# A graph-attention layer's last chunks: four of them smaller, one more of them, and their softmax chain in one piece

## What is computed

```python
def _gat_layer(x, src, dst, edge_attr_full, W, att, b, ew, eb):
    edge_emb = edge_attr_full @ ew.T + eb
    xw = x @ W
    xj = xw[src].reshape(-1, H, D) + edge_emb.reshape(-1, H, D)
    xi = xw[dst].reshape(-1, H, D)
    alpha = jnp.einsum('ehd,hd->eh', xi, att_i) + jnp.einsum('ehd,hd->eh', xj, att_j)
    alpha = jax.nn.leaky_relu(alpha, NEG_SLOPE)
    amax = jax.ops.segment_max(alpha, dst, num_segments=N)
    ea = jnp.exp(alpha - amax[dst])
    denom = jax.ops.segment_sum(ea, dst, num_segments=N)
    alpha = ea / (denom[dst] + EPS)
    msg = xj * alpha[..., None]
    aggr = jax.ops.segment_sum(msg, dst, num_segments=N)
    return aggr.mean(axis=1) + b
```

## Time and profile before

| | |
|---|---|
| median of three runs | 3343.92 us |
| the profiled execution's own time | 3336.89 us |
| its span, first to last instruction | 3335.0 us |
| TensorE busy | 2402.9 us, 72% of the span |
| GpSimd busy | 2172.8 us, 65% |
| VectorE busy | 2021.6 us, 61% |
| ScalarE busy | 669.5 us, 20% |
| the chain that ended last: GpSimd, VectorE, TensorE, issue, DMA | 30%, 28%, 22%, 13%, 4% |

### The profile page before, as it was taken

How to read it: one execution, slowest core, us unless ns; L and a number is a source line. 1 busy time by engine, 2 the same in 40 slices (tenths; PEclk the granted TensorE clock), 3 DMA queues, 4 the chain that set the end, 5 groups by cost and what they waited for, 6 DMA issues and landing times.

```text
span 3335.0 us, 48601 instructions
## 1 busy us (share of the span) xinstructions
PE 2402.9 (72%) x13595; PEld 1979.9 (59%) x13595; DVE 2021.6 (61%) x6441; ACT 669.5 (20%) x3102; POOL 2172.8 (65%) x2357
## 2 busy tenths in 40 slices
PE   6879955777675677668477777747777685777668
PEld 6669924566564566556366565636556573556557
DVE  8965464665565565656655665755665574665557
ACT  0048921111114111110411111131111122111112
POOL 0047737777755777774677777377777737777772
PEclk9555555555557555555755555575555566555556
DMA  3211112222221222221222222122222212222221
GB/s 100 102 66 68 46 55 59 60 61 58 63 48 43 58 63 58 58 64 40 50 63 58 58 67 56 33 59 61 58 60 64 56 35 57 60 60 58 58 55 50
DMA packets 114123, 195.78 MB, mean 59 GB/s; under 512 B 39898, under 2 KB 77273, under 8 KB 113865
## 3 DMA queue, kind: packets, MB, share of 16 engines
q0 software_dynamic: 62560, 130.25, 17.4%
q1 hardware_dynamic: 51304, 62.42, 5.9%
HBM read 180.86 MB, written 11.67 MB: 58 GB/s over the span
## 4 chain that ended last, share of the span: by engine, by line
POOL 30%; DVE 28%; PE 22%; issue 13%; DMA 4%; DVEq 2%; ACT 1%; POOLq 0%; ACTq 0%
POOL ring L510 28%; PE bank L745 10%; PE bank L747 5%; DMA ring<-table,srci 4%; DVE acc L1208 2%; PE bank L718 2%; DVE into L1149 2%; PE bank L741 2%; DVE prod L1072 2%; DVE ring L847 2%; DVE lanes L1135 2%; DVE fwd L1156 1%; POOL ring L491 1%; PE bank L783 1%; DVEq L1016 1%
## 5 line engine op out<-in xcount | busy, mean ns | idle before, releaser
L510 POOL DMA_INDIRECT ring<-table,srci x1955 | 1903.9, 974 | 633.1 <-issue 571.4
L745 PE MATMUL bank<-pw,ring 128*128 128x48 f32 x3910 | 1216.9, 411 | 0.0
L745 PEld LDWEIGHTS bank<-pw,ring 128*128 128x128 f32 x3910 | 1009.1, 316 | 103.8 <-issue 23.9
L741 PE MATMUL bank<-zeros 128*128 128x288 bf16 x490 | 209.6, 428 | 622.0 <-DVE pw L1167 622.0
L747 PE MATMUL bank<-onehot,est 128*36 128x24 f32 x3910 | 619.1, 246 | 0.0
L747 PEld LDWEIGHTS bank<-onehot,est 128*36 128x36 f32 x3910 | 382.6, 150 | 177.5
L586 ACT ACTIVATE dd<-dd 128x66 f32<-128x66 f32 x75 | 19.4, 258 | 2152.2 <-DVE dd L1160 2152.2
L741 PEld LDWEIGHTS bank<-zeros 128*128 128x128 bf16 x490 | 54.3, 111 | 665.3 <-DVE pw L1167 630.7
L1111 DVE TENSOR_TENSOR alpha<-alpha,ring 128x56 f32<-128x56 f32 (+7 forms) x75 | 18.1, 241 | 702.6 <-DMA ring<-table,srci 702.4
L1208 DVE TENSOR_TENSOR acc<-acc,bank 128x288 f32 x490 | 222.4, 454 | 301.7 <-PE bank L747 183.0
L580 ACT COPY ai_win<-ai_rows 128x48 f32 x1955 | 309.1, 228 | 58.0 <-issue 22.7
(11 more groups left out here) (214 smaller groups left out, 2676.1 us busy)
## 6 DMA issues: line engine op xcount, KB each, us to landing
ring<-table,srci POOLq DMA_INDIRECT x1955
ai_rows<-lo_dram SPq DMA_DIRECT2D x28, 896.0 KB, 4.3
at<-in_attr SPq DMA_DIRECT2D x65, 224.0 KB, 2.5
table<-ring SPq DMA_DIRECT2D x15, 390.0 KB, 3.6
table<-ring SPq DMA_DIRECT2D x5, 325.0 KB, 3.3
result<-ring SPq DMA_DIRECT2D x24, 64.0 KB
x_mid<-ring SPq DMA_DIRECT2D x3, 384.0 KB, 2.7
table<-ring SPq DMA_DIRECT2D x5, 130.0 KB, 2.3
```

The lines of the kernel that those rows point to most:

```text
L510: nc.gpsimd.indirect_dma_start(out=ring[:, slot(t), :], out_offset=None, in_=table, in_offset=bass.IndirectOffsetOnAxis(ap=srci[:, t:t + 1 ...
L741: nc.tensor.matmul(total, zeros[:, 0:P], zeros[:, :], start=True, stop=False, skip_group_check=True)
L745: nc.tensor.matmul(wide[:, 0:H, at_k], ring[:, slot(t), 0:D], pw[:, g % DEEP, k, :, :], start=False, stop=False, skip_group_check=True)
```

## The change

The list of chunks becomes eleven of 28 tiles and then 24, 20, 16, 12 and 11, sixteen in all; the number of groups stays 98. The ring has 59 slots, since the flags of one more chunk need the room of one. `FULL` is 11, the first smaller chunk. While chunks 0 to 10 are worked on, the order on VectorE is as before. In chunks 11 to 14 all of `windows_sum` for the next chunk runs ahead of add 0, and its chain runs in one piece ahead of the third add from the end, that is behind 3, 2, 1 and 0 adds. The chain's end then weighs three groups of chunks 12 to 15, and the end of the chunk the fourth where there is one. `ROW_BLOCKS` has six blocks in place of three.

```diff
-CH = [K] * 13 + [16, 11]
+CH = [K] * 11 + [24, 20, 16, 12, 11]
 NC = len(CH)
+FULL = CH.count(K)
...
-RING = 60
+RING = 59
...
-def chain_at(c):
-    return (2, 3, 5) if len(GC[c]) >= 7 else (0, 1, len(GC[c]) - 2)
+CHAIN = (2, 3, 5)
+
+
+def chain_before(c):
+    return len(GC[c]) - 3 if c >= FULL else None
+
+
+def weighed_early(c):
+    return 2 if c <= FULL else min(3, len(GC[c]))
...
-        ROW_BLOCKS = [(0, 13, K), (13, 14, CH[13]), (14, 15, CH[14])]
+        ROW_BLOCKS = [(0, FULL, K)] + [(c, c + 1, CH[c]) for c in range(FULL, NC)]
...
-                for g in GC[c][0:2 if c else AHEAD]:
+                for g in GC[c][0:weighed_early(c) if c else AHEAD]:
                     weigh(layer, g)
...
-                    scan_at, rows_at, probs_at = chain_at(c)
+                    scan_at, rows_at, probs_at = CHAIN if chain_before(c) is None else (None, None, None)
                     n_groups = len(GC[c])
                     for i, g in enumerate(GC[c]):
-                        if more and scan_at >= 2 and i < 3:
+                        if more and scan_at is not None and i < 3:
                             windows_sum(layer, c + 1, i)
+                        if more and scan_at is None and i == 0:
+                            for part in range(3):
+                                windows_sum(layer, c + 1, part)
+                        if more and i == chain_before(c):
+                            chain_scan(layer, c + 1)
+                            chain_rows(layer, c + 1)
+                            chain_cols(layer, c + 1)
+                            chain_probs(layer, c + 1)
                         add_group(layer, g)
...
-                        if more and scan_at < 2 and i == 0:
-                            for part in range(3):
-                                windows_sum(layer, c + 1, part)
...
-                            for ahead in GC[c + 1][2:AHEAD]:
+                            for ahead in GC[c + 1][weighed_early(c + 1):AHEAD]:
                                 weigh(layer, ahead)
```

## The result

The changed kernel takes 3308.01 us (median of four runs, 3305.78 to 3308.75) against 3344.14 for the kernel before: ratio 0.9891, 95% interval 0.9874 to 0.9908, 36.1 us less. The forecast was 3304, the range 3295 to 3318. The profiled execution takes 3305.78 us, its span is 3303.9.

What follows compares the result with a forecast made beforehand. GpSimd's gathers set the pace, but the change reaches each layer's tail, a string of VectorE work: 8.3 us a layer, 41.6 over five, less 1.5 for slower gathers, 40.1 off, so 3304 us against the median; range 3295 to 3318.

Steps and rivals of the forecast that it cites:

- the tail: End of each layer, last gather to last add: 31.99 us in layer 1, forecast to fall to near 23.7.
- VectorE's string: Layer 1 from chunk 13's landing at 947.55: VectorE's work alone sets the last add, 997.5, 8.3 us before 1005.84.
- The rival of a tail that does not move: End of each layer: held adds stop TensorE, or the last chain still starts near 985.7; 3344 us, 4%.
- half of the gain: Rival for the whole kernel: a mixture, with only half of the forecast saving, 3324 us; 4%.
- The sum: Whole kernel: 41.6 us saved over five layers less 1.5 is 40.1 us off 3336.89, giving 3296.8.
- gathers beside a denser VectorE: One more chain lies under gathers: charged 0.3 us a layer, 1.5 in all; bounds 0 and 4.2 a layer.
- The rival of the gathers slowed by 4.2 us a layer: VectorE's copies lock GpSimd out of the port, delaying every landing: 21 us in all, 3323 us; 8%.
- VectorE a chunk behind: Rival at chain 13: VectorE comes to it late, so the 16th chunk is added work; 16 us slower, 3360; 6%.
- The offset to the median: Kernel before: its profiled execution, 3336.89, is 7.0 us below the median 3343.92; carried over, 3296.8 becomes 3304.
- Ring 59: Gathers ask for slots one tile, 1.25 us, sooner; some 20 us cover it, else up to 1.25 us a layer.
- SP's row loads: Prologue: 36 issues become 72, with 2.8 us of cover for the look-up copy; taken as 0, bounds 0 and +2 us.
- The held adds: Chunks 11 to 14: adds held behind the chain keep PSUM, but six banks suffice, so TensorE goes on; no cost.

Runs made afterwards that it cites:

- the early and late doubling: Changed kernel with the second window-sum reduction run three times: early for chunks 12 and 13, 3305.91 us; late for chunks 14 and 15, 3320.26 us.
- side by side: No edit: the changed kernel and the kernel before, measured again in one series on one chip: 3306.21 against 3344.51 us, ratio 0.9886.
- the sizes alone: New chunk sizes and ring of 59 with the old order on VectorE, against the kernel before: 3339.13 us, ratio 0.9983.
- the copies beside gathers: Changed kernel with four extra SBUF copies of 128 x 672 float32 in VectorE's wait ahead of the chains of chunks 1 to 10: 3317.89 us, one execution.
- the wait put to use: Changed kernel with the first two parts of chunk 14's window sums, and ScalarE's copies for them, moved ahead of chain 13: 3298.24 us, ratio 0.9857.
- the shorter order alone: Changed kernel with the old sizes and ring of 60, so only chunk 13's loop has the new order: 3331.15 us, ratio 0.9963 against the kernel before.

## Why the prediction was right

- **The bound and the place.** GpSimd paces, the tail is VectorE's string, it begins at chunk 13's landing: shown by the early and late doubling. The rival of a tail that does not move is out (39.40 to 31.35 us of idle time), and so is that of half the gain.
- **The string's terms**, forecast and then measured in layer 1: chain 12 9.3 and 9.34; chain 13 9.12 and 9.06; weighings, adds, weighing and rescale 3.40 and 3.40 (958.92 to 962.32); sums of chunk 14 with its one add 4.03 and 4.35 (to 966.67); chain 14 8.6 and 8.86; 3.13 and 3.15; sums of chunk 15 2.93 and 2.93; chain 15 8.65 and 8.52; 0.41 and 0.41; 9.67 and 9.67. From chunk 13's landing to the last add 49.95 and 50.35. The largest miss is the add ahead of chain 14, for which I took the 0.56 us of idle time seen ahead of other adds; it has 0.91, ended by TensorE's sum. The next is chain 14, 0.26 us.
- **The sum.** The tail gave 40.6 us where the forecast had 41.6. The medians gave 36.1 and 38.3 in two series, where I had 40.1. The profiled pairs put the tail at 40.6 and 41.1, so the missing 2 to 4 us are not in the tail; the gathers' pace, which moved one execution by 11 us, is large enough for them, but the executions at the medians were not profiled. The range has a slip: 1.3 us a layer are 6.5 us, so 3297.5 to 3310.5, where I wrote 3296 to 3312; the time lies in either.
- **A wrong term that cost little.** I charged 1.5 us for gathers beside a denser VectorE; side by side the gathers are 1.6 us shorter in sum, so the term is nothing that can be told. The reason given for it was the smaller half: I looked to the chain's copies, and two-input instructions do more. In layer 1 of the changed kernel the long gathers of 1.01 and 1.09 us at 943.45 and 963.54 lie beside the window sums' products of two inputs (from 943.09 and 962.99), not beside a chain. The rival of the gathers slowed by 4.2 us a layer is out, and so is that of VectorE a chunk behind: chain 13 waits 2.18 us where I had 1.5.
- **The offset to the median.** Taking the 7.0 us over was right, but I gave no reason for it. The profiled execution of the changed kernel came at 3305.78, 9 us above the 3296.8 of the sum, because its gathers did not have the quick pace of the one I started from (1912.8 and 1903.9 us).
- **Cover at no cost.** Ring 59 and SP's row loads cost nothing, each as forecast; SP took 29.69 us for 72 issues, 0.41 each, where I had 32.4. The held adds cost nothing either: each of TensorE's four waits ends with a weighing, none with a bank.
- Most of the experiments' forecasts held too. Those that did not are the sizes alone, 5 us instead of 12, since the loss of a late chain adds to the next; the copies beside gathers, 12.5 us in the gathers' sum where one theory had 30 or more and the other none; and in part the wait put to use, where the tail gave 5 of 7 us.

## What to carry to other kernels

Where an engine paces a stage, price the stretch behind its last instruction by itself: find the last wait that the second engine still has on it, and add that engine's own work from there to the end; before that wait work is free and can be moved to, as long as it does not slow the pacing engine itself; behind it nothing is. Smaller last pieces each bring their fixed work with them, so shorten that work first, or together: here the sizes alone gave 5 us, the shorter order alone 13, both 38. Before two profiled executions are compared term by term, run the old kernel beside the new one and compare the pace of what neither changes: here one quick execution hid 9 of 41 us.

## What the runs showed of the hardware

Gathers issued by GpSimd are held up by VectorE instructions that read two tensors in SBUF, 0.29 us for each microsecond of them, more than by float32 copies with one input (0.12). The Trainium skill (SBUF — State Buffer, "Who interferes with whom") expects copies to stall such gathers and infers that `tensor_tensor` does not, since it shares only the read side of the port with GpSimd; here the measurement decides against that inference. The same section says that an instruction with two SBUF inputs contends with a GpSimd instruction that reads SBUF, and these gathers take their indices from a tile in SBUF (`srci`). Whether it is that read which waits was not tried.

A granted clock in a view has to be held against the matmuls. For the stretch from 190 to 475 us (columns: length; busy us and count of PE, PEld, DVE, ACT, POOL; PEclk; DMA share; GB/s) the first profiled execution of the changed kernel shows a granted clock of 1.00, the one of the series 0.50, with the same busy times:

```profile
190.00:475.00 285.00, 235.32 (x2037) 218.90 (x2036) 165.23 (x511) 197.86 (x648) 172.04 (x166) 1.00 0.18 58
```

```profile
190.00:475.00 285.00, 235.22 (x2037) 218.82 (x2035) 165.21 (x511) 197.91 (x648) 172.03 (x166) 0.50 0.17 58
```

That looks as if TensorE's small matmuls there took as long at 2.4 GHz as at 1.2. The rows show no such thing. Four larger matmuls near the end of the stretch, and four of the same form behind it, in the first execution and then in the other:

```profile
468.52 3.78 PE L774 MATMUL bank<-S,V 128*128 128x512 f32 x4 [6.53 <-ACT S L607]
...
475.67 1.88 PE L774 MATMUL bank<-S,V 128*128 128x512 f32 x4
```

```profile
468.39 3.78 PE L774 MATMUL bank<-S,V 128*128 128x512 f32 x4 [6.53 <-ACT S L607]
...
475.53 1.88 PE L774 MATMUL bank<-S,V 128*128 128x512 f32 x4
```

In the second execution the granted clock is 0.50 (1.2 GHz) at the first four and 1.00 (2.4 GHz) at the others, and they take 3.78 and 1.88 us. In the first execution the same four take the same 3.78 us, so its clock at 468 us was the lower one too. The trace of that execution has no clock record before 473.7 us, and the view counts time without a record as 1.00. What the small matmuls would take at 2.4 GHz, no run here shows.
